# Expert weights of a grouped mixture-of-experts stage: one 3 MB DMA after the down matmuls in place of a 2 MB and a 1 MB DMA

## What is computed

```python
def _moe_group(x2, router_w, wg, wu, wd, top_k):
    scores = jax.nn.softmax(x2 @ router_w, axis=-1)
    expert_weights, expert_indices = lax.top_k(scores, top_k)
    ...
    xs = x2[tok]                                   # sorted by expert
    gate = lax.ragged_dot(xs, wg, group_sizes)
    up = lax.ragged_dot(xs, wu, group_sizes)
    ys = lax.ragged_dot(jax.nn.silu(gate) * up, wd, group_sizes)
    ys = ys * flat_w[order][:, None]
    return jnp.zeros_like(x2).at[tok].add(ys)
out = (out0 * TOP_K + out1 * TOP_K) / (TOP_K + TOP_K)
```

## Time and profile before

| what | value |
|---|---|
| median of 2 runs | 5342.54 us (5341.21 to 5343.87) |
| the profiled execution | 5324.93 us |
| its span, first to last instruction | 5323.2 us |
| mean granted TensorE clock | 0.934 |

### The profile page before, as it was taken

One profiled execution on the slowest core, in us unless ns is written; L12 is line 12 of the kernel. 1 busy time (PEld: TensorE's weight loads), 2 busy tenths in 40 slices (PEclk: granted clock), 3 DMA queues, 4 the chain that ended last, 5 costly groups with the idle time before them and its releaser, 6 DMA issues.

```text
span 5323.2 us, 87131 instructions
## 1 busy us (share of the span) xinstructions
PE 4653.1 (87%) x22649; PEld 3828.8 (72%) x22649; DVE 3203.5 (60%) x6155; ACT 1616.5 (30%) x3933; POOL 2832.0 (53%) x2173
## 2 busy tenths in 40 slices
PE   6979787879797978378988888899999999999999
PEld 4767676767676767356777777777778888888887
DVE  6879797979797979544444444445434444444444
ACT  2333333333333333222332322233222222222222
POOL 2566666666666666534444444445445555555554
PEclk8989898989898989689999999999999999999999
DMA  5454545454545353489999999999898888888887
GB/s 209 145 143 145 146 142 147 142 148 140 150 138 151 137 153 136 119 290 299 313 290 314 310 316 264 296 319 321 222 281 239 237 241 250 230 244 238 213 236 203
DMA packets 370053, 1152.07 MB, mean 216 GB/s; under 512 B 50257, under 2 KB 50258, under 8 KB 351138
## 3 DMA queue, kind: packets, MB, share of 16 engines
q0 software_dynamic: 182512, 454.27, 35.3%
q1 hardware_dynamic: 145842, 544.24, 30.0%
q10 hardware_dynamic: 41472, 151.01, 7.6%
HBM read 719.35 MB, written 463.57 MB: 222 GB/s over the span
## 4 chain that ended last, share of the span: by engine, by line
PE 33%; DMA 17%; issue 4%; POOL 1%; DVE 1%; POOLq 0%; SPq 0%; ACT 0%; DVEq 0%; ACTq 0%
DMA out<-c_yo,c_idx 16%; PE ps L1293 10%; PE ps L1295 10%; PE ps L1294 9%; PE ps L1302 3%; PE ps L1321 1%; DMA c_xg<-h2g_d,c_idx 1%; POOL out L1282 1%; POOL c_xg L1254 1%; DVE c_yo L1537 1%; DMA c_wt<-wsp_d 0%; POOLq L1274 0%; DVE c_xl L1525 0%; DMA wsp_d<-c_stg 0%; POOL c_lists L1266 0%
## 5 line engine op out<-in xcount | busy, mean ns | idle before, releaser
L1282 POOL DMA_INDIRECT out<-c_yo,c_idx x576 | 917.0, 1592 | 1373.8 <-DMA out<-c_yo,c_idx 605.1
L1293 PE MATMUL ps<-c_wt,c_xh 128*128 128x512 f32 x2304 | 967.9, 420 | 39.7 <-issue 21.5
L439 PE MATMUL ps<-xTh,wTh 128*128 128x512 f32 x1536 | 648.8, 422 | 334.9 <-DVE xTl L808 242.9
L1295 PE MATMUL ps<-c_wt,c_xl 128*128 128x512 f32 x2304 | 913.1, 396 | 0.0
L1294 PE MATMUL ps<-c_wt,c_xh 128*128 128x512 f32 x2304 | 908.4, 394 | 0.0
L1537 DVE SCALAR_TENSOR_TENSOR c_yo<-ps,c_wc,c_xg 128x512 f32<-128x512 f32 x576 | 432.5, 751 | 663.4 <-DMA out<-c_yo,c_idx 399.1
L1521 DVE TENSOR_TENSOR c_hh<-ps,c_sil 128x256 f32<-128x256 f32 x576 | 243.8, 423 | 861.2 <-ACT c_sil L1373 817.6
L1254 POOL DMA_INDIRECT c_xg<-h2g_d,c_idx x576 | 576.1, 1000 | 180.6 <-issue 148.1
L1378 ACT CAST c_xh<-ps 128x512 fp32r<-128x512 f32 x576 | 337.7, 586 | 1074.4 <-PE ps L1302 1001.7
L440 PE MATMUL ps<-xTl,wTh 128*128 128x512 f32 x1536 | 629.6, 410 | 0.0
L441 PE MATMUL ps<-xTh,wTl 128*128 128x512 f32 x1536 | 628.4, 409 | 0.0
(11 more groups left out here) (196 smaller groups left out, 7847.1 us busy)
## 6 DMA issues: line engine op xcount, KB each, us to landing
c_wt<-wsp_d SPq DMA_DIRECT2D x69, 2048.0 KB
c_wt<-wsp_d SPq DMA_DIRECT2D x69, 1024.0 KB
sraw<-wex SPq DMA_DIRECT2D x97, 512.0 KB
wsp_d<-shigh SPq DMA_DIRECT2D x96, 512.0 KB
wsp_d<-sraw SPq DMA_DIRECT2D x96, 512.0 KB
c_stg<-wex ACTq DMA_DIRECT2D x96, 512.0 KB
wsp_d<-c_sgh ACTq DMA_DIRECT2D x96, 512.0 KB
wsp_d<-c_stg ACTq DMA_DIRECT2D x96, 512.0 KB
```

What stands on the lines that cost most here:

```text
L439: nc.tensor.matmul(o, lh, rh, start=first, stop=False)
L1282: nc.gpsimd.indirect_dma_start(out=out, out_offset=bass.IndirectOffsetOnAxis(ap=idx[:, n:n + 1], axis=0), in_=yo[:, n % 4, :], in_offset=N ...
L1293: nc.tensor.matmul(o, lh, rh, start=first, stop=False)
L1295: return nc.tensor.matmul(o, ll, rh, start=False, stop=last)
```

## The change

The two semaphores of a buffer become one. SP waits once for each slot, for `y_done` of slot n - 4, and then issues one DMA over the whole 24 KB of each partition, 3 MB in all. PE waits for that one DMA ahead of `gate_up`, and `down` has no wait for weights of its own. Bytes, buffers and the order of PE's work stay.

```diff
-        w_gu, w_d = ([sem(f"{n}{u}") for u in range(W)] for n in ("w_gu", "w_d"))
+        w_in = [sem(f"w_in{u}") for u in range(W)]
...
-                loads = ((w_gu[u], gu_done, 0, GU), (w_d[u], y_done, GU, GU + 2 * HC * C))
+                loads = ((w_in[u], y_done, 0, GU + 2 * HC * C),)
...
             for u in range(W):
-                sp.wait_ge(w_gu[u], 16 * (SLOTS // W))
-                sp.wait_ge(w_d[u], 16 * (SLOTS // W))
+                sp.wait_ge(w_in[u], 16 * (SLOTS // W))
...
                 pe.wait_ge(x_lo, cp(it, s))
-                pe.wait_ge(w_gu[u], rnd(it, s, W))
+                pe.wait_ge(w_in[u], rnd(it, s, W))
...
                 pe.wait_ge(h_lo, cp(it, s))
-                pe.wait_ge(w_d[u], rnd(it, s, W))
```

## The result

The change made the kernel slower: 5538.82 us median (5536.24 to 5541.39, 2 runs) against 5342.54, ratio 1.036 with a 95% interval of 1.0335 to 1.0385. That is 196 us; 206 were forecast, and the range 5425 to 5660 holds it.

A forecast was written before the change was run, and what follows sets the result against it. The early half was taken as bound by the DMA engines, the late half by PE. Terms 143 + 5 + 2 + 56 = 206 us on the 5342.5 us median gave 5548 us, 8-in-10 range 5425 to 5660.

The forecast's parts named there:

- Room: Isolated late switches: from the new load's issue to the unstalled start of gate_up there are 9.0 us.
- Duration: Late switches: the 3 MB load takes 12.7 us till PE goes on, bounds 12.2 to 15.0, so PE stalls 3.7 us.
- Price of a stall: Late switches: a 3.7 us stall costs 5.3 us, with 1.6 for the lowered clock, as read at slot 166.
- Count: Late half: 27 of 37 switches stall, leaving out five in a row and five seconds of close pairs.
- Late term: Stalls ahead of gate_up at late switches: 27 x 5.3 = 143 us in the forecast's sum.
- Slots 256 to 292: Five switches in a row around slot 288: the load queue sets the pace, +5 us for all five.
- First four slots: First loads: the last must land 3 MB and not 2, at most +3.3 us, taken as +2.
- Early half: Stalls move from down to gate_up: +2 us for each of 28 switches, 56 us, bounds 0 to 196.
- Rival 1: Early half: weight stalls come on top of the adds' stall, 140 to 196 us, total 5630 to 5690; chance 0.17.
- rival 2: Late switches: 3 MB take 11 us, PE idles 2 us with the clock kept, 89 us, total 5432; chance 0.08.
- rivals 3 and 4: Weight waits: load lands in time, 5335 to 5343 us, chance 0.04; one fixed DMA cost less, 5335 us, chance 0.01.
- Rival 4: Switches: one DMA's start and completion less, at most 7.0 us of PE's waits at L1293, 5335 us; chance 0.01.

The follow-up runs named there:

- e3: The changed kernel with two DMAs of 2 and 1 MB in place of one, both after y_done of slot n - 4, gate_up waiting for both; 5572.4 us.
- e10: The kernel before with each staging store on ACT cut into two DMAs of 2 KB rows; 5327.7 us, ratio 0.9979.
- e1: The kernel before with both loads issued after y_done of slot n - 4, gate_up and down keeping a wait each; 5400.5 us, ratio 1.0111.
- e5: The kernel before without the staging of the second group's weights; 5133.2 us, ratio 0.961.
- e6: The changed kernel without the staging of the second group's weights; 5403.1 us, ratio 1.011 to the kernel before.
- e2: The kernel before with its two DMAs issued where they were, but gate_up waiting for both; 5401.3 us, ratio 1.0120.

## Why the prediction was right

The forecast was 206 us and 196 came, by the mechanism and nearly the steps it gave. That the sum is so close is in part luck: the late half's term was 25 us too small and the early half's 27 us too large, and the load's duration came near for a reason that the prediction didn't give.

- *Room, 9.0 us:* 8.97 at slot 440, 9.06 as the median of 31 late switches. Right.
- *Duration, 12.7 us, bounds 12.2 to 15.0:* 13.1 by packets. The stall was 3.94 us of idle time where 3.7 was forecast; bounds held. The number was taken near the lower end on the ground that PE's stall stops gathers and adds, and that one DMA takes what the pair took. Neither is borne out: the pair of the kernel before took 13.6 us as the median of the late switches (the example, slot 366, was one of the fastest), and the pair of e3, with a stall beside it, took 14.3. What brought the load back to 13.1 is the merging, which the prediction put at 0 among its parts; without it the whole would have cost 230 us (e3), still inside the range.
- *Price of a stall, 5.3 us:* 162.9 / 27 = 6.0. Of the 0.7 missing, 0.2 is the longer hole and 0.5 what comes beyond it: 2.1 us where slot 166 had shown 1.6. The prediction called all of this the clock; 0.25 us of it stands between the idle time and the late start, with the clock kept too (slot 366: 2.23 us idle, 2.49 us late).
- *Count, 27:* 27 waits, with one swap. One of the 27 foreseen, slot 272, lies ahead of the stretch that the waits cover, so 26 were due in it. The other is slot 368, second of a pair two slots apart, foreseen without a stall: slot 366 stalled so briefly (2.23 us, clock kept) that it left too little room. The other four such pairs had none.
- *Late term:* foreseen 26 x 5.3 = 138 us in the late half, measured 162.9. The sum's one term that was too small.
- *Slots 256 to 292:* foreseen 5 + 5.3 (slot 272), 10.3 us; 191.0 became 200.4, 9.4. *First four slots:* +2 foreseen; from the first load's issue to `gate_up(4)` the time fell by 1.6 us, from 49.1 to 47.5, but it was 45.7 us in e10 and 50.4 in e1, where nothing in it is changed, so no gain or loss is shown.
- *Early half, +56 us:* +28.9, 1.0 us for each switch and not 2. The step was right in kind (waits moved from `down` to weights, and the staging covered most of the cost, as e5 and e6 show) and its size was taken too large. It lay within the bounds of 0 and 196.
- The rest of the span's 211.3 us is 11.6 us ahead of the first weight load (2287.6 against 2276.0 us) where nothing was changed; other kernels with the same first stage issue it between 2276.4 and 2284.9. The profiled execution of the kernel before was 17.6 us below its median, and the medians' 196 is the better number.

The rule of the Trainium skill that spoke against a stall, "DMA: Bandwidth & Descriptors" (Anatomy of one DMA), would give 9.2 us for 3 MB, an estimate by its fit of 2.0 us plus bytes / 436 GB/s for DMAs that GpSimd issues. This load is issued by SP, and it took 13.1 us beside gathers and adds; no run here has it alone. Rival 1 (early stalls on top) is excluded by +28.9 us, rival 2 (short stalls, clock kept) by holes of 3.94 us and the late half's 0.96, rivals 3 and 4 by the 27 waits. Rival 4's idea, that one DMA less is worth something, is true in another way: 34 us by e3, by a shorter load and not by a saved wait.

## What to carry to other kernels

Before joining two loads, write down for each when its buffer is free and when its first reader comes: the joint load starts at the later of the one and is due at the earlier of the other. Here that cut the room from 12.1 to 9.1 us and raised what must land in it from 2 to 3 MB, and either alone cost about a third of what the change cost. The stall to expect is duration less room, with the duration taken beside the traffic it will meet, plus what the clock takes afterwards; in the half where the DMA engines were the bound, 29 us of it showed, where 110 did without the staging.

## What the runs showed of the hardware beyond that

- A hole costs more than its length even far apart from others: 106.5 us of holes made the late half 162.9 us longer, 1.5 times, with the lower clock behind 23 of 27; in e2, where they were 1.4 us each, 38.2 us made 48.2, 1.3 times, with the lower clock behind 2 of 28. The length of a hole alone doesn't tell whether the clock falls: of two of 2.23 us in the changed kernel it fell behind one (slot 375) and stayed behind the other (slot 366).
- One 3 MB load with 24 KB rows landed in 13.1 us, the same bytes as 16 KB and 8 KB rows, issued 1.5 us apart, in 14.3, and as six loads with 4 KB rows (issued within 4.0 us, from another place in the slot) in 17.5, each beside the same adds and gathers. Row length and number of DMAs were not separated.
- Equal loads in a steady stretch differ in duration by up to 2.5 us: of 31 loads of 3 MB four landed in 11.1 to 11.3 us and the others in 12.1 to 13.6, for a reason that these runs don't give.
